# A GNN and transformer stack on one core: the remainder at the end of the next block, norm and degrees inside the build, the result stored in 120 and 5 rows

## The reference, cut to what matters

```
edge_index = stack([src, dst])
x = x + L0_gnn(layernorm(x), edge_index, ...)      # two SAGE convolutions
x = x + L0_ffn(layernorm(x), ...)                  # attention, 64 experts
x = x + L1_gnn(layernorm(x), edge_index, edge_weight)
x = x + L1_ffn(layernorm(x), ...)
x = x + L2_gnn(layernorm(x), ...)                  # three GCN layers, batch norm
x = x + L2_ffn(layernorm(x), ...)                  # eight experts
x = x + L3_gnn(layernorm(x), ...)
x = x + L3_ffn(layernorm(x), ...)                  # attention, 8 experts, top 2
return x

def layernorm(x): (x - mean) / sqrt(var + 1e-5)    # over the 512 values of a row
def sage_conv(x, src, dst, Wl, bl, Wr):            # L0_gnn
    summed = segment_sum(x[src], dst)
    cnt = segment_sum(ones, dst)
    return summed / maximum(cnt, 1) @ Wl.T + bl + x @ Wr.T
```

## Time and profile before

| what | us |
|---|---|
| median of 3 runs (3237.39 to 3237.93) | 3237.43 |
| the profiled execution's own time | 3236.85 |
| its span | 3235.0 |
| span: DVE makes its first one-hot tile (L265) | 29.29 |
| span: the last remainder ends | 400.4 |
| span: first SAGE product begins (L1895) | 431.65 |
| span: the last addition to x ends | 3218.0 |

### The profile page before, as it was taken

How to read it: one execution, slowest core, us unless ns; L and a number is a source line. 1 busy time by engine, 2 the same in 40 slices (tenths; PEclk the granted TensorE clock), 3 DMA queues, 4 the chain that set the end, 5 groups by cost and what they waited for, 6 DMA issues and landing times. The chain is left out here.

```text
span 3235.0 us, 40132 instructions
## 1 busy us (share of the span) xinstructions
PE 2629.9 (81%) x12039; PEld 1818.8 (56%) x12040; DVE 1690.7 (52%) x3404; ACT 1039.2 (32%) x2287; POOL 278.9 (9%) x273
## 2 busy tenths in 40 slices
PE   5778779957999976999598789958877579998874
PEld 2334346545787744665274466656635367777552
DVE  7898821255888725444534432331133378886343
ACT  2555520023667710111301122211111247776110
POOL 0000000000000002443000000002300000000031
PEclk9999989978999987999798899959979789998777
DMA  3000041011000027896502400034250110000344
GB/s 106 26 16 16 16 114 45 17 45 31 20 19 19 13 58 239 304 304 200 132 14 119 90 14 13 1 114 147 69 124 9 47 36 20 19 16 16 102 126 110
DMA packets 113648, 238.20 MB, mean 74 GB/s; under 512 B 32600, under 2 KB 33960, under 8 KB 112230
## 3 DMA queue, kind: packets, MB, share of 16 engines
q10 hardware_dynamic: 42608, 116.92, 12.7%
q1 hardware_dynamic: 46582, 91.71, 9.6%
q0 software_dynamic: 24320, 27.90, 3.0%
HBM read 189.78 MB, written 52.58 MB: 75 GB/s over the span
## 5 line engine op out<-in xcount | busy, mean ns | idle before, releaser
L309 PE MATMUL ps<-onehot_src,onehot_dst 125*128 x1140 | 257.6, 358 | 81.3 <-ACT stage_hi L367 36.6
L1171 DVE TENSOR_REDUCE mx<-ps 125x1 f32<-125x500 f32 (+1 forms) x480 | 274.1, 589 | 56.6 <-PE ps L941 40.1
L1066 ACT ACTIVATE probs_hi<-ps 125x500 fp32r<-125x500 f32 (+1 forms) x480 | 254.9, 531 | 123.4 <-DVE probs_lo L1123 82.2
L1123 DVE TENSOR_TENSOR probs_lo<-x,probs_hi 125x1250 fp32r<-125x1250 f32 x160 | 241.1, 1507 | 34.7 <-ACT x L1068 31.2
L1068 ACT ACTIVATE x<-ps 125x500 f32<-125x500 f32 (+1 forms) x480 | 257.5, 537 | 0.0
L1815 DVE COPY yb<-ps 78x512 f32<-78x512 f32 (+1 forms) x100 | 68.8, 688 | 321.4 <-PE ps L1752 321.4
L265 DVE TENSOR_SCALAR onehot_src<-iota,src_f 125x1250 f16 x380 | 206.1, 542 | 37.5 <-PE ps L309 27.8
L309 PEld LDWEIGHTS ps<-onehot_src,onehot_dst 125*128 x1140 | 105.7, 101 | 210.1 <-issue 156.2
L1752 PE MATMUL ps<-w2s,hT 128*78 128x512 f32 (+1 forms) x480 | 216.4, 597 | 1.9 <-ACT hT L1777 1.9
L941 PE MATMUL ps<-K_hi_lo,Q_hi_twice 128*125 128x500 f32 (+1 forms) x480 | 181.1, 383 | 22.8 <-DVE mx L1171 17.6
L949 PE MATMUL ps<-Q_hi_twice,K_hi_lo 128*125 128x500 f32 (+1 forms) x480 | 178.9, 373 | 17.8 <-ACT Q_lo_max L1056 5.1
(11 more groups left out here) (378 smaller groups left out, 4847.0 us busy)
## 6 DMA issues: line engine op xcount, KB each, us to landing
room<-in_L_ffn_w_p ACTq DMA_DIRECT2D x63, 512.0 KB, 5.5
w2s<-in_L_ffn_w ACTq DMA_DIRECT2D x63, 512.0 KB, 7.1
G<-c_spill ACTq DMA_DIRECT2D x2, 5859.4 KB
tv<-in_L_ffn_tv_W_p SPq DMA_DIRECT2D x2, 4096.0 KB
w_spill<-weight_rows ACTq DMA_DIRECT2D x10, 585.9 KB
c_spill<-CT ACTq DMA_DIRECT2D x1, 5859.4 KB
slabs<-w_spill SPq DMA_DIRECT2D x10, 585.9 KB
w1s<-in_L_ffn_w_p ACTq DMA_DIRECT2D x5, 1024.0 KB, 4.8
```

Of the source, the lines that this page charges most:

```text
L309: mm_ = pe.matmul(ps[:, 3 * half + c, 0:cn], ohd[:, slot, :].rearrange("p o n -> p (o n)"), ohs[:, slot, c0:c0 + cn].rearrange("p o n -> p ...
L1066: act.activation(PH[:, t % 2, c0:c0 + cn], ps[0:P, ST + n, 0:cn], ACT.Exp, scale=SCALE).then_inc(p_hi, 1)
L1123: v.tensor_tensor(PL[:, t % 2, :], PT[:, t % 2, :], PH[:, t % 2, :].bitcast(fp32), ALU.subtract)\
L1171: v.tensor_reduce(mx[:, t, n:n + 1], ps[0:P, SQ + cc % 2, 0:cn], AX.X, ALU.max)\
```

## The change

It does four things.

1. The remainder of window w-1 is called at the end of window w's tiles, in place of that of w-2 behind the second tile.
2. The degrees, their roots, and the first layernorm (statistics, root, scaling) move into the build's block, on DVE behind the last remainder. The turns of the last group get a place of their own ((0, 1)), so that ACT takes the two roots between the last sums and the turns. x is waited for by its own semaphore.
3. The first SAGE weights are loaded by SP right behind x at the start of the build. The block behind the build is now `transpose_only`; SP issues the counts' way to DRAM at its start.
4. The result is stored in DMAs of 120 and 5 rows, even row tiles by SP and odd ones by ACT.

```diff
-                  "end": {(0, 0): (0, sums(2, (0, 1, 2)) + sums(3, (0, 1, 2)) + turns(0, 1, 2))}}
+                  "end": {(0, 0): (0, sums(2, (0, 1, 2)) + sums(3, (0, 1, 2))), (0, 1): (6, turns(0, 1, 2))}}
...
                         for t in range(HEAD):
                             onehots(first + t, before + t, base)
-                            if t == 1 and (j >= 2 or where != "first"):
-                                remainder(w - 2, (j - 2) % WPT)
                         with v.Fori(0, runs) as r:
                             for h in range(RUN):
                                 onehots(first + RUN * r + (HEAD + h), before + RUN * r + (HEAD + h), base)
+                        if j or where != "first":
+                            remainder(w - 1, (j - 1) % WPT)
...
                 schedule(v, group)
-                remainder(NW - 2, WPT - 2)
                 remainder(NW - 1, WPT - 1)
+
+                v.wait_ge(x_in, 32)
+                for i in range(T):
+                    v.bn_stats(k.stats[:, i, :], x[:, i, :]).then_inc(x_stats, 1)
+                v.wait_ge(x_stats, T)
+                for i in range(T):
+                    v.bn_aggr(mv[:, i, :], k.stats[:, i, :]).then_inc(x_stats, 1)
+                v.wait_ge(x_stats, 2 * T)
+                v.tensor_scalar(sd[:, :], mv[:, :, 1], 1e-5, None, ALU.add).then_inc(var_ready, 1)
+
+                s = Steps(v, end_steps)
+                v.wait_ge(aux_out, chunk(T, "end", 5) * 2 + 6)
+                s.did(v.tensor_reduce(cols[:, 2, :], deg[:, :, :].rearrange("p c t -> p t c"), AX.X, ALU.add))
+                s.wait()
+                v.tensor_scalar(cols[:, 0, :], cols[:, 2, :], 1.0, None, ALU.add).then_inc(deg1, 1)
+                s.did(v.tensor_scalar(cols[:, 2, :], cols[:, 2, :], 1.0, None, ALU.max))
+                s.wait()
+                v.reciprocal(k.inv_deg[:, :], cols[:, 2, :])
+
+                v.wait_ge(std_ready, 1)
+                v.reciprocal(rs[:, :], sd[:, :]).then_inc(inv_ready, 1)
+                v.wait_ge(inv_ready, 1)
+                for i in range(T):
+                    v.tensor_scalar(x[:, i, :], x[:, i, :], mv[:, i, 0:1], rs[:, i:i + 1], ALU.subtract, ALU.mult)
+                v.wait_ge(root_done, 1)
+                v.reciprocal(k.dinv[:, :], cols[:, 1, :])
...
-                aux(T, 0, "end", None, 0, 0, sum_parts, turn_counts)
+                for slot in range(2):
+                    aux(T, 0, "end", None, 0, slot, sum_parts, turn_counts)
...
                 aux(T, 0, "end", None, 0, 0, take_sums, take_counts)
+                act.wait_ge(var_ready, 1)
+                act.activation(sd[:, :], sd[:, :], ACT.Sqrt).then_inc(std_ready, 1)
+                act.wait_ge(deg1, 1)
+                act.activation(cols[:, 1, :], cols[:, 0, :], ACT.Sqrt).then_inc(root_done, 1)
+                aux(T, 0, "end", None, 0, 1, take_sums, take_counts)
...
+            if spill:
+                @block.sync
+                def _(sp):
+                    for dst, src, done in spill:
+                        sp.dma_start(dst, src).then_inc(done, 16)
...
+            def store(eng, first):
+
+                for t in range(first, T, 2):
+                    eng.wait_ge(added, K_ * (t + 1))
+                    for to, what in in_two(out[P * t:P * t + P, :], x[:, t, :]):
+                        eng.dma_start(to, what).then_inc(out_stored, 16)
...
                 if out is not None:
-                    for t in range(T):
-                        sp.wait_ge(added, K_ * (t + 1))
-                        sp.dma_start(out[P * t:P * t + P, :], x[:, t, :]).then_inc(out_stored, 16)
-                    sp.wait_ge(out_stored, 16 * T)
+                    store(sp, 0)
+                    sp.wait_ge(out_stored, 32 * T)
...
                     loads(act, 1)
+                if out is not None:
+                    store(act, 1)
...
-        norm_rows(nc, k, x, x, hT, beside=weights(0),
-                  later=[(to, what, c_out) for to, what in in_two(rowtiles(c_spill), G[:, :, :].bitcast(fp32))])
+        transpose_only(nc, k, x, hT, spill=[(to, what, c_out) for to, what in
+                                            in_two(rowtiles(c_spill), G[:, :, :].bitcast(fp32))])
...
-                spill_rows(sp, x, rowtiles(a["x"]), start_done)
-                n = 32
+                spill_rows(sp, x, rowtiles(a["x"]), x_in)
+                for dst, src in l0_weights(a, first, 0):
+                    sp.dma_start(dst, src).then_inc(start_done, 16)
+                n = 48
```

More of the change, by code:

```diff
@@ L45, in wait, with build_graph @@
         self.eng.wait_ge(self.sem, self.base + self.n)
[L48 removed]
+def build_graph(nc, k, CT, w_spill, src_pt, dst_pt, w_pt, dst_rows, scr_minmax, scr_tab, beside, x, x_in):
     SLOTS = 8
@@ L399, in _ @@
                 aux(T, 0, "end", None, 0, 0, take_sums, take_counts)
+                act.wait_ge(var_ready, 1)
[3 more added lines that the diff above has]
+                aux(T, 0, "end", None, 0, 1, take_sums, take_counts)
                 for s_ in w_out:
                     act.wait_ge(s_, 32 + 32 * (T // 2))
[L403 to L421, removed]
-                v.reciprocal(k.dinv[:, :], cols[:, 1, :])
 class Kit:
@@ L561, in copy_transposed, with transpose_only @@
             g += 1
-def transpose_only(nc, k, xn, xT, beside=()):
+def transpose_only(nc, k, xn, xT, beside=(), spill=()):
     with k.semaphore(nc, k.name("loaded")) as loaded, k.semaphore(nc, k.name("transposed")) as transposed, \
@@ L1901, in row_terms, with l0_weights, l0_gnn @@
     return [(lhsT[:, c, P * i:P * i + P], rhs[:, c, :]) for lhsT, rhs, n in terms for c in range(n)]
-def l0_gnn(nc, k, a, x, G, c_spill, c_out):
+def l0_weights(a, to, l):
+    wl, wr, bl = to
+    return [(wl[:, :, :], kchunks(a[f"L0_gnn_Wl{l}T"])), (wr[:, :, :], kchunks(a[f"L0_gnn_Wr{l}T"])),
+            (bl[:, :], a[f"L0_gnn_bl{l}"].partition_broadcast(P))]
+def l0_gnn(nc, k, a, x, G, c_spill, c_out, first):
     with ExitStack() as ctx:
@@ L1909, in l0_gnn @@
         hT = sb("hT", [128, C, N])
-        wl, wr, bl = sb("wl", [128, C, D]), sb("wr", [128, C, D]), sb("bl", [P, D])
+        wl, wr, bl = first
         own = sb("own", [P, T, D])
         u = pair_of(nc, k, ctx, "u", [P, T, D])
-        def weights(l):
-            return [(wl[:, :, :], kchunks(a[f"L0_gnn_Wl{l}T"])), (wr[:, :, :], kchunks(a[f"L0_gnn_Wr{l}T"])),
-                    (bl[:, :], a[f"L0_gnn_bl{l}"].partition_broadcast(P))]
         def relu(v, i):
@@ L1922, in add_the_relu @@
             return v.scalar_tensor_tensor(x[:, i, :], own[:, i, :], 0.0, x[:, i, :], ALU.max, ALU.add)
-        norm_rows(nc, k, x, x, hT, beside=weights(0),
-                  later=[(to, what, c_out) for to, what in in_two(rowtiles(c_spill), G[:, :, :].bitcast(fp32))])
+        transpose_only(nc, k, x, hT, spill=[(to, what, c_out) for to, what in
+                                            in_two(rowtiles(c_spill), G[:, :, :].bitcast(fp32))])
         sage_layer(nc, k, hT, wl, wr, bl, G, u, own, relu)
-        transpose_only(nc, k, x, hT, beside=weights(1))
+        transpose_only(nc, k, x, hT, beside=l0_weights(a, first, 1))
         sage_layer(nc, k, hT, wl, wr, bl, G, u, own, add_the_relu, x, in_two(x, rowtiles(a["x"])), c_out)
@@ L2529, in program @@
         x = x128[0:P]
-        start_done = ctx.enter_context(k.semaphore(nc, "start_done"))
+        start_done, x_in = (ctx.enter_context(k.semaphore(nc, n)) for n in ("start_done", "x_in"))
         def scratch(name, shape, dt=fp32):
@@ L2543, in program @@
         CT = counts.enter_context(nc.sbuf_tensor("CT", [P, T, N], f32r))
+        first = [counts.enter_context(nc.sbuf_tensor(n, shape, fp32))
+                 for n, shape in (("wl", [128, C, D]), ("wr", [128, C, D]), ("bl", [P, D]))]
         with ExitStack() as c2:
@@ L2567, in beside @@
                 sp.wait_ge(start_done, n)
-            build_graph(nc, k, CT, w_spill, a["src_pt"], a["dst_pt"], a["w_pt"], a["dst_rows"], scr1, scr2, beside)
+                sp.wait_ge(x_in, 32)
+            build_graph(nc, k, CT, w_spill, a["src_pt"], a["dst_pt"], a["w_pt"], a["dst_rows"], scr1, scr2, beside, x, x_in)
         k.clear_semaphores(nc)
-        l0_gnn(nc, k, a, x, CT, c_spill, c_out)
+        l0_gnn(nc, k, a, x, CT, c_spill, c_out, first)
         counts.close()
```

4 lines of the change are left out of this document (added).

## The result

The changed kernel took 3215.19 us in the median of its runs (3212.69 to 3218.23), the kernel before 3237.68 beside it; the ratio of the runs is 0.9925, 95% interval 0.9911 to 0.9939. The medians differ by 22.5 us; by the ratio it is 3237.68 x 0.0075 = 24.3 us. The kernel before now had one run at 3245.22 beside three that agree to 0.02%, so such an agreement of three says little of the spread. The forecast was 3213.1, its range 3203 to 3221. The profiled execution took 3213.30 us with a span of 3211.5, 23.5 less than the 3235.0 of before.

What follows compares the result with a forecast made beforehand. PE was busy 81% overall, PE and DVE waited for each other in the build, and stores ended the kernel. Gains of 1.5 + 8.8 + 14.0 = 24.3 us off 3237.4 gave 3213.1 us, range 3203 to 3221.

Steps and rivals of the forecast that it cites:

- G1: Build: moving the remainder forward shortens PE's waits at the three jumps back; taken as 1.5 us.
- the choice between the bounds: Build, three jumps back: waits give 0 to 4.0 us; +1.5 taken, near the side where PE's own jump sets the start.
- the sign named for it: Build: the window start behind each jump stays near 2.9 us; a fall to 1.6 would show the first rival.
- the ends, -3 and +8 us: Build: the outer bounds put on the gain from the remainder's new place, around the +1.5 us taken.
- the first rival: Build: it gains in full, with window starts behind the jumps falling to 1.6 us; chance 0.17.
- G2: Last remainder to first SAGE product: norm and degrees in the build bring the product 8.8 us sooner, bounds 7 and 11.
- G3: Kernel's end: storing the result in 120 and 5 rows saves 14.0 us, bounds 9 and 15.5.
- the term behind the last addition: Kernel's end: from 3217.99, an issue of 0.35, about 2 us to landing and 0.7 added, giving 3221.0.
- the later of two limits: Kernel's end: moving the result's bytes, to 3218.9, or last addition plus issue and landing, 3220.3; the later counts.
- The build losing to the clock: Build: the rival that the build loses to the clock; chance 0.12.
- Last loads held up: Kernel's end: early stores beside the loads delay the last piece by 4 to 5 us; G3 = 9, 3218.1; chance 0.13.
- Slower by DVE's short lead: Build: remainder ahead of the first tile delays PE up to 0.9 us over 39 windows, 35 us, 3249.8; chance 0.02.

Runs made afterwards that it cites:

- e9: The changed kernel with 16 small bf16 matmuls at each window's start and two waits moved ahead of the table reading; ratio to the kernel before 0.9894, build 356.9 us.
- e8: The changed kernel with the 4.65 us row scaling moved from the build's block into the transposes' block; ratio to the kernel before 0.9907.
- c1: The changed kernel run once more with no edit; ratio to the kernel before 0.9908, build 366.0 us.
- e7: The changed kernel with all stores, in 120 and 5 rows, issued by SP; no ratio, last loads' issue to end 32.4 us against 33.7.
- e11: The changed kernel with small matmuls at each window's start and the remainder back in its old place; ratio to the kernel before 0.9938, build 364.4 us.
- e4: The changed kernel with the first SAGE weights issued by SP after 12 windows are summed; ratio to the kernel before 0.9907.
- e3: The changed kernel with the remainder back in its old place; median 3215.7 us, ratio to the kernel before 0.9928.
- e5: The changed kernel with a loop of two turns over 16 windows in place of four over 8; ratio to the kernel before 0.9917, build 368.7 us.

## Why the prediction was right, point by point

The places and the mechanisms of all three parts were right, and the time, 3215.2 against 3213.1, is close. Part of that closeness is luck: in the profiled execution the parts missed by +1.5, +0.7 and -2.1 us and the start of the build by -1.0, and these nearly cancel to 23.5 against 24.3.

- **The remainder's place (G1, 1.5 us; measured 3.0 in the profiled build, 7.1 on the average of the profiles).** The right places were named, the three jumps back, and that the new wait for ACT's copy costs nothing: in the profile after, L281 waits for it once, 5.0 us for the last window, where nothing else is left to do, as it did before. The step that failed is the choice between the bounds: the likeness of the three gaps (2.93 us on average) was taken as a sign that PE's own jump sets them, and the sign named for it, starts that stay near 2.9, did not come. PE's jump allows 2.1 us, and the old 2.9 were the remainder behind DVE's standstill. Worth 0.8 each, 2.4 us, where 1.33 each was the most. The clock's part in the ends, -3 and +8 us, and in the first two rivals was the author's estimate, and no run shows it: with the new place no build had more stretches at the lower clock, they were four fewer on average, 7.6 against 11.7, and by e9 a stretch costs PE about 1.5 us and the build 1.0 us. In e9, with small matmuls in PE's idle starts, none was left. So the first rival, a gain of 9 us in the build, was nearer to the average than the forecast; the first profile happened to have the longest build of the seven.
- **Norm and degrees in the build (G2, 8.8; measured 9.5 here, 9.2 on the average: 30.9 us in the three profiles with the old norm, 21.8 in the nine with the change but without e8's edit).** Right in each step to 0.1 us up to the start of the transposes. From there to the product it took 7.84 us, not 8.4: PE was granted 0.73 of its clock in them, not 0.67, and ACT was free from the first on; in c1 the clock was 0.65 and the same way took 8.56 us. Moving the norm and loading the weights early were never separated: the weights were put at nothing because they hide under the build, and in the profile after nothing is seen to wait for them, but no run has the one without the other. The table load took 1.28 us in the profile after, and the root began 1.30 us behind its start, on an engine that had been busy 0.75 us before, so 2.05 us lie between ACT's last work and the root.
- **The stores (G3, 14.0; measured 11.9 here, 13.0 on the average: the three profiles with 125 rows have 45.7 in the mean, the eleven with 120 and 5 rows 32.7).** The cause was right: the rows decide, with a DMA share of 0.33 and 127 GB/s for stores of 125 rows and of 0.98 and 355 GB/s for those of 120 and 5. Mis-sized was the term behind the last addition, 3.0 us: 4.4 in this profile and 4.3 to 4.4 in the ten others with these stores. That is 1.4 of the 2.1 us; the other 0.7 came ahead of it, since the last addition ended 29.3 us behind the loads' issue in place of 28.6, inside the spread of 26.5 to 30.1 over all profiles. In the first 2 us behind it the engines were still 0.77 busy with stores of earlier tiles (253 GB/s), bytes flowed until about 3210, and the span ended 1.5 us after. The prediction let only the later of two limits count, the moving of the bytes and the last addition; here the last row tiles' stores still stood behind earlier ones, so the two add in part.
- **Nothing else moved**: 2757.8 and 2757.7 us from the product to the last loads. The 1.0 us at the start is chance (29.0 to 30.6 over the profiles).
- **The rivals.** The build losing to the clock: it went the other way, fewer stretches and not more. Last loads held up: not seen (26.3 us behind their issue against 25.6 in this pair, but 25.5 on the average of the ten profiles with the new stores in which DVE waited for them, against 25.7 in the three without). Slower by DVE's short lead: no sign; where the remainder was ahead of the first tile a tile of DVE's was named as the releaser more often (30 times against 15), but ordinary starts stayed at 1.6 us.

The sum of the averages is 7.1 + 9.2 + 13.0 = 29.3 us. The changed kernel was timed twice, with 24.3 us by its first ratio and 3238.2 x 0.0092 = 29.8 by c1's, and the two intervals overlap; the sum meets the second and lies just above the first's interval (19.7 to 28.8).

## What to carry to other kernels

Look at what ends a kernel: here stores of 125 rows in one DMA ran for 15 us behind the last addition at a DMA share of 0.33 (127 GB/s), and a cut into 120 and 5 rows took 13 us off, from one queue (e7) as from two. Where two engines run in step, look for the places where the lead is gone before pricing the rest: here the order of the remainder was worth 0.8 us behind each of the loop's jumps, and ordinary starts stayed at 1.6 us. And a short idle that repeats can have a second price in TensorE's clock: here 16 tiny matmuls in each window's start took away all of the 6 to 10 stretches at a clock of 0.50 and 7.8 us of one stage (e9), but where they stood behind a late wait (e11) the starts grew to 3.7 to 4.1 us and two such stretches were left.

## What the runs showed of the hardware that had not been expected

- Behind a jump back over eight windows DVE stood still for 2.5 to 4.0 us (2.49 in e4, 4.03 in e3), and with the new place of the remainder PE's start there took 2.1 us in place of 1.6; behind the one over sixteen windows in e5 it took 5.2 us once.
- With packets of 2 KB either way, the DMA engines moved 219 GB/s at a share of 0.99 while the last loads ran and 355 GB/s at 0.98 when mostly stores ran (and 127 at 0.33 with stores alone). Whether the direction or the side that is read makes the difference is not told apart.
- Low-clock stretches in the build mostly stand at the long window starts, 8 of 11 in the kernel before and 7 of 10 in the changed one; the others stand at ordinary starts of 1.6 us. They are not at the same places from execution to execution (6 to 10 with the same place of the remainder), and with them the build took from 362.1 to 368.1 us.
